# Cross-attention with keys on the partitions: a pass for the maximum, then keys and V as stationary operands in tiles of the array

## The reference, cut to what matters

```python
# x: (2, 1024, 256), context: (2, 154, 256), mask: (2, 154); H = 16 heads of HD = 16
q = split_heads(layernorm(x) @ q_w.T + q_b)
k = split_heads(context @ k_w.T + k_b)
v = split_heads(context @ v_w.T + v_b)
scores = einsum('bhqd,bhkd->bhqk', q, k) / sqrt(HD)
scores = where(mask, -inf, scores)
probs = softmax(scores)
x = x + einsum('bhqk,bhkd->bhqd', probs, v)   # heads side by side again
```

## Time and profile before

| | us |
|---|---|
| median of 3 executions | 926.87 (916.11 to 928.25) |
| profiled execution | 923.59 |
| its span in the trace | 921.8 |
| cross-attention stage, from the first `queries` to the last `head_o` | 500.1 to 690.2 |
[...]

### The profile page before, as it was taken

One profiled execution on the slowest core, in us unless ns is written; L12 is line 12 of the kernel. 1 busy time (PEld: TensorE's weight loads), 2 busy tenths in 40 slices (PEclk: granted clock), 3 DMA queues, 4 the chain that ended last, 5 costly groups with the idle time before them and its releaser, 6 DMA issues.

```text
span 921.8 us, 13568 instructions
## 1 busy us (share of the span) xinstructions
PE 768.8 (83%) x4214; PEld 572.5 (62%) x4215; DVE 508.3 (55%) x1135; ACT 322.0 (35%) x685; POOL 263.9 (29%) x236
## 2 busy tenths in 40 slices
PE   1978661999998684887799999999998479999996
PEld 1733221676766422533366788888888469999995
DVE  5388888565565459223323766666653544444442
ACT  1355642121222220012244655566552022233220
POOL 2754347777776420300000000000000023222231
PEclk9798785899999786778957999999995579999999
DMA  5000001111112162000000000000009201110110
GB/s 173 1 0 0 0 0 34 35 52 34 51 51 52 49 249 116 0 0 0 3 0 1 6 14 12 12 11 11 12 12 325 92 23 33 37 38 30 34 30 1
DMA packets 36210, 37.72 MB, mean 41 GB/s; under 512 B 4648, under 2 KB 32621, under 8 KB 36173
## 3 DMA queue, kind: packets, MB, share of 16 engines
q1 hardware_dynamic: 32956, 32.11, 10.6%
q0 software_dynamic: 2208, 5.12, 1.9%
q10 hardware_dynamic: 1008, 0.03, 0.1%
HBM read 26.77 MB, written 5.11 MB: 35 GB/s over the span
## 4 chain that ended last, share of the span: by engine, by line
PE 61%; issue 16%; DVE 12%; POOL 5%; ACT 3%; DMA 1%; DVEq 0%; SPq 0%; POOLq 0%; ACTq 0%
PE pair L1843 9%; PE bank L1854 9%; PE bank L1736 6%; PE pair L1711 5%; PE bank L1618 4%; PE bank L1724 4%; PE bank L1700 3%; DVE arena L901 3%; PE pair L1433 3%; POOL arena L424 2%; PE bank L1744 2%; PE bank L1807 1%; PE bank L1408 1%; DVE ybuf L1001 1%; POOL arena L409 1%
## 5 line engine op out<-in xcount | busy, mean ns | idle before, releaser
L1433 PE MATMUL pair<-featT,ybuf 128*128 (+1 forms) x128 | 64.9, 666 | 25.3 <-DVE arena L890 24.9
L1182 DVE TENSOR_REDUCE xmax<-pair 128x4 f32<-128x616 f32 x64 | 51.1, 798 | 60.8 <-PE pair L1711 60.8
L1854 PE MATMUL bank<-arena,prob_b 128*128 x368 | 83.1, 379 | 0.0
L1843 PE MATMUL pair<-ybuf 128*128 128x128 f32 x560 | 81.0, 281 | 0.0
L901 DVE SCALAR_TENSOR_TENSOR arena<-arena,conv_w 128x512 f32<-128x512 f32 x72 | 71.5, 1055 | 10.4 <-ACT arena L590 10.3
L1843 PEld LDWEIGHTS pair<-ybuf 128*128 128x128 f32 x560 | 74.5, 198 | 1.1
L505 POOL TENSOR_TENSOR xres<-xres,ybuf 128x256 f32 x16 | 11.6, 724 | 219.1 <-DVE ybuf L1199 219.1
L1854 PEld LDWEIGHTS bank<-arena,prob_b 128*128 128x128 f32 x368 | 68.2, 190 | 8.3
L792 ACT ACTIVATE prob_b<-pair,gate_w 128x128 f32<-128x128 f32 x92 | 26.2, 368 | 117.4 <-PE pair L1843 117.4
L1433 PEld LDWEIGHTS pair<-featT,ybuf 128*128 128x128 f32 x128 | 27.2, 217 | 61.6 <-issue 34.2
L1736 PEld LDWEIGHTS bank<-arena,ybuf 122*128 122x128 f32 x512 | 62.2, 192 | 0.0
(11 more groups left out here) (352 smaller groups left out, 1634.4 us busy)
## 6 DMA issues: line engine op xcount, KB each, us to landing
arena<-W1T SPq DMA_DIRECT2D x8, 1024.0 KB, 12.4
arena<-W2T SPq DMA_DIRECT2D x8, 1024.0 KB, 12.0
arena<-arena SPq DMA_DIRECT2D x16, 384.0 KB, 3.1
xres<-x SPq DMA_DIRECT2D x4, 512.0 KB, 6.6
x_rows<-xres SPq DMA_DIRECT2D x16, 128.0 KB, 1.7
ybuf<-attn_in_wT SPq DMA_DIRECT2D x1, 1288.0 KB, 11.6
featT<-b SPq DMA_DIRECT2D x8, 128.0 KB, 4.7
w_out<-attn_out_wT SPq DMA_DIRECT2D x1, 512.0 KB, 13.0
```

Of the source, the lines that this page charges most:

```text
L1182: dve.tensor_reduce(mx.rearrange("p (a h) -> p a h", a=2), sc, AX, ALU.max).then_inc(S("score_max"), 1)
L1433: m = pe.matmul(bank[f % 5][:, :], w_in[:, k, f * P:(f + 1) * P], featT[:, k, ds(blk * BLK, BLK)], start=(k == 0), stop=(k == KD - 1))
L1843: m = pe.matmul(bank[2 * p + half][:, f * P:(f + 1) * P], w1_now[k][p][:, (4 * half + f) * P:(4 * half + f + 1) * P], xsT[:, p, k, :], sta ...
L1854: m = pe.matmul(bank[4 + p][:, 0:D], hidT[:, p, f, :], w2_of[:, ds(e * NFF + f, 1), :].rearrange("p a n -> p (a n)"), start=(f == 0), stop ...
```

## The change

The maximum is found in a pass of its own. Then the scores are computed a second time with keys as the stationary operand, so that they come out with keys on the partitions, where the weighing needs them; the transposes of probabilities and their copies go. The maximum enters as one more row of the contraction: `neg_max` (the former buffer's column HD + 1, times a constant row of -4 in the key's bias and a scale of 0.25) is transposed and added to the queries, so the second scores are already shifted. Exp reads PSUM directly. V is stationary in 32-column tiles of the array; the output has head columns on the partitions, and is transposed back. `keys` is no longer block-diagonal, so a score matmul uses a 32-row tile of the array, one head each. The tile loops are unrolled in the program text. Some semaphores are merged with shared counters (`dve_once`), which leaves their order as it was.

The diff's core:

```diff
-        pair = [ctx.enter_context(nc.psum_tensor(f"pair{i}", [P, 2, 512], F32)) for i in range(2)]
+        quad = ctx.enter_context(nc.psum_tensor("quad", [P, 4, 512], F32))
-        keys = cut([B, NG, GH * LK])
-        v_main = cut([B, XH, HD + 1])
-        v_tail = cut([B, NG, GH * (HD + 1)])
+        keys = cut([B, NG, LK])
+        key_tail = cut([B, NG, P])
+        v_main = cut([B, XH, 32])
+        v_tail = cut([B, NG, P])
@@ SyncE
-            sp.wait_ge(S("prob_turned"), (NG + 1) * NT)
+            sp.wait_ge(S("pv_mm"), NT)
@@ GpSimd, ahead of the stage
+            pool.memset(bias_rows[:, 1, :, HD + 1:HD + 2], -4.0).then_inc(pool_once, reached("bias_rows_cleared_1"))
+            pool.wait_ge(S("keys_ready"), B * NG)
+            for h in range(GH):
+                r = slice(32 * h, 32 * h + 32)
+                if h:
+                    pool.wait_ge(S("key_tail_ready"), h)
+                pool.tensor_copy(key_tail[r, :, :, 32 * h:32 * h + KT], keys[r, :, :, KM:LK]).then_inc(S("key_tail_ready"), 1)
@@ ScalarE: keys in 8 operations instead of 32, then
+            def exp_scores(t):
+                act.wait_ge(S("main_mm"), t + 1)
+                act.activation(prob_m[0:KM, :, :, :].rearrange("p h g n -> p h (g n)"), quad[0:KM, :, :], ACT.Exp).then_inc(S("prob_m_ready"), 1)
+                act.wait_ge(S("tail_mm"), t + 1)
+                act.activation(prob_t, bank[5][:, :].rearrange("p (g n) -> p g n", g=NG), ACT.Exp).then_inc(S("prob_t_ready"), 1)
+            def keep_o(t):
+                act.wait_ge(S("pv_mm"), t + 1)
+                if t:
+                    act.wait_ge(S("o_turned"), t)
+                act.activation(oT, bank[6][:, :], ACT.Copy).then_inc(S("oT_ready"), 1)
+            for t in range(NT):
+                if t + 2 < NT:
+                    keep_q(t + 2)
+                if t:
+                    keep_o(t - 1)
+                exp_scores(t)
@@ VectorE
+            def max_scores(t, half):
+                dve.wait_ge(S("score_x_mm"), 2 * t + half + 1)
+                for_half = max_cols[:, 2 * half:2 * half + 2, :, HD + 1]
+                dve.tensor_reduce(for_half.rearrange("p g h -> p h g"), quad[:, :, 0:2 * LK].rearrange("p h (g n) -> p h g n", g=2), AX, ALU.max
+                                  ).then_inc(S("score_max"), 1)
+            def add_max(t):
+                dve.wait_ge(S("max_turned"), t + 1)
+                q = qT[:, t % 3, :, :].rearrange("p g n -> p (g n)")
+                dve.tensor_tensor(q, q, bank[7][:, :], ALU.add).then_inc(S("qmax_ready"), 1)
+            # weigh(t): waits o_turned, reads bank[4]; reciprocal and product as before
+            for t in range(NT):
+                if t + 1 < NT:
+                    max_scores(t + 1, 0)
+                    max_scores(t + 1, 1)
+                    add_max(t + 1)
+                if t >= 1:
+                    weigh(t - 1)
+                if t >= 2:
+                    row_stats(t - 2)
@@ TensorE
             def queries(t):
+                if t >= 4:
+                    pe.wait_ge(S("head_o_ready"), t - 3)
+                # 8 matmuls into bank[4]
+            def scores(t, half):
+                if half == 0:
+                    pe.wait_ge(S("qT_ready"), t + 1)
+                    if t >= 2:
+                        pe.wait_ge(S("prob_m_ready"), t - 1)
+                else:
+                    pe.wait_ge(S("score_max"), 2 * t + 1)
+                for i in range(2):
+                    for h in range(GH):
+                        r = slice(32 * h, 32 * h + 32)
+                        m = pe.matmul(quad[:, h, i * LK:(i + 1) * LK], qT[r, t % 3, 2 * half + i, :], keys[r, t // TB, 2 * half + i, :],
+                                      start=True, stop=True)
+            def turn_max(t):       # 4 transposes of neg_max into bank[7]
+            def scores_by_key(t):
+                pe.wait_ge(S("qmax_ready"), t + 1)
+                pe.wait_ge(S("score_max"), 2 * (t + 1) + 2)
+                for g in range(NG):
+                    for h in range(GH):
+                        r = slice(32 * h, 32 * h + 32)
+                        m = pe.matmul(quad[0:KM, h, g * P:(g + 1) * P], keys[r, t // TB, g, 0:KM], qT[r, t % 3, g, :], start=True, stop=True)
+                for g in range(NG):
+                    m = pe.matmul(bank[5][:, g * P:(g + 1) * P], key_tail[:, t // TB, g, :], qT[:, t % 3, g, :], start=True, stop=True)
+            def weigh(t):          # waits prob_m_ready, prob_t_ready, oT_ready
+                for g in range(NG):
+                    pe.matmul(bank[6][:, g * P:(g + 1) * P], v_tail[:, t // TB, g, :], prob_t[:, g, :], start=(g == 0), stop=False,
+                              skip_group_check=True)
+                for g in range(NG):
+                    for h in range(GH):
+                        m = pe.matmul(bank[6][32 * h:32 * h + 32, g * P:(g + 1) * P], v_main[0:KM, t // TB, GH * g + h, :],
+                                      prob_m[0:KM, h, g, :], start=False, stop=True, skip_group_check=True)
+            def turn_out(t):       # waits oT_ready, qT_ready, head_o_ready; 4 transposes of oT into bank[4]
+            queries(0)
+            queries(1)
+            scores(0, 0)
+            scores(0, 1)
+            turn_max(0)
+            for t in range(NT):
+                if t + 1 < NT:
+                    scores(t + 1, 0)
+                if t + 2 < NT:
+                    queries(t + 2)
+                if t + 1 < NT:
+                    scores(t + 1, 1)
+                if t:
+                    weigh(t - 1)
+                scores_by_key(t)
+                if t + 1 < NT:
+                    turn_max(t + 1)
+                if t:
+                    turn_out(t - 1)
+            weigh(NT - 1)
+            turn_out(NT - 1)
```

More of the change, by code:

```diff
@@ L94, in reached @@
             return 1
-        pair = [ctx.enter_context(nc.psum_tensor(f"pair{i}", [P, 2, 512], F32)) for i in range(2)]
-        bank = [pair[i // 2][:, i % 2, :] for i in range(4)]
+        quad = ctx.enter_context(nc.psum_tensor("quad", [P, 4, 512], F32))
+        bank = [quad[:, i, :] for i in range(4)]
         bank += [ctx.enter_context(nc.psum_tensor(f"bank{i}", [P, 512], F32)) for i in range(4, 8)]
@@ L751, in _ @@
-            keep_q(0, 0)
-            def tile_step(t, p, now=True, before=True, waits=True, nxt=True):
-                for g in range(NG):
-                    if nxt and g == 1:
-                        keep_q(t + 1, 1 - p)
-                    if before:
-                        keep_probT(t - 1, g, waits)
-                    if before and g == NG - 1:
-                        keep_probT(t - 1, NG, waits)
-                    if now:
-                        exp_scores(t, p, g)
-            tile_step(0, 0, before=False)
@@ L1276, in _ @@
             link(dve.tensor_reduce(best, hot, AX, ALU.max))
[L1277 removed]
+            dve.tensor_tensor(hot, across(desc, NT), along(best, NE), ALU.is_equal).then_inc(dve_once, reached("hot_ready"))
             link(dve.memset(before[:, 0, :], 0.0))
@@ L1701, in queries @@
                                       start=(k == 0), stop=(k == KD - 1))
                 m.then_inc(S("q_mm"), 1)
-            def scores(t, p, g, waits, b):
-                if waits:
-                    pe.wait_ge(S("shifted"), NG * t + g - 1)
-                if g == 0:
+            def scores(t, half):
+                if half == 0:
                     pe.wait_ge(S("qT_ready"), t + 1)
-                for j in range(2):
-                    r = slice(64 * j, 64 * j + 64)
-                    m = pe.matmul(pair[g % 2][:, j, 0:2 * LK], qT[r, p, g, :],
-                                  keys[r, b, g, 2 * j * LK:(2 * j + 2) * LK], start=True, stop=True)
-                m.then_inc(S("score_x_mm"), 1)
@@ L1730, in weigh_main @@
-            def weigh_main(t, p, g, waits):
-                pe.wait_ge(S("probT_ready"), (NG + 1) * t + g + 1)
-                if g == 0 and waits:
-                    pe.wait_ge(S("head_o_ready"), t - 1)
-                for h in range(GH):
-                    hh = GH * g + h
-                    m = pe.matmul(bank[6 + p][:, hh * W:(hh + 1) * W], probT[0:KM, hh, :],
-                                  vm_of[0:KM, ds((t // TB) * XH + hh, 1), :].rearrange("p a n -> p (a n)"), start=(hh == 0), stop=False,
-                                  skip_group_check=True)
-                m.then_inc(S("pv_mm"), 1)
```

218 lines of the change are left out of this document (75 added, 143 removed).

## The result

| | before | after |
|---|---|---|
| median | 924.91 us (916.11 to 928.25) | 891.17 us (890.72 to 892.75) |
| profiled execution, its span | 923.59, 921.8 | 891.23, 889.5 |
| attention stage, first `queries` to last `head_o` | 190.1 | 157.9 |
| one tile in the steady stretch | 11.68 | 8.90 |
| mean granted TensorE clock of the span, as a share of full speed | 0.874 | 0.879 |

Four executions of each kernel (the median before of three, with which the forecast worked, was 926.87); the ratio is 0.9653, with a 95% interval of 0.9582 to 0.9723. The change makes the program 33.7 us faster. The two spans differ by 32.3: the stage gives 32.2 of it, the part before it took 1.7 more (it begins at 501.87 instead of 500.13) and the part behind it 1.8 less. So the gain is the stage's, as it should be.

What follows compares the result with a forecast made beforehand. PE was taken to bound the attention stage. Its pieces summed to 9.06 us per tile, 9.4 with waits, against 11.68; with the ends this gained 28.9 us, so 926.87 - 28.9 = 898.0, range 885 to 940.

Steps and rivals of the forecast that it cites:

- The bound: Attention stage: PE alone sets the time, 11.68 us per tile before; work taken from VectorE or ScalarE gains nothing by itself.
- The prices: PE's work per tile after the change, priced piece by piece from earlier rows: 9.06 us against 11.68.
- 8 sets of 0.14: V's and keys' tiled matmuls: four tiles overlap, 8 x 0.14 + 0.21 = 1.3 us each per tile.
- Maximum and exponential: VectorE's maximum over 1232 elements takes 1.44 us, ScalarE's exp of 2048 columns 1.9, both extended from shorter operations.
- The waits: Steady tile: queries wait 0.2 us for `head_o`; next scores wait for exp, making the cycle 9.4 us.
- The ends: Fill and drain of the stage: second round starts at about 518.9, last round and drain take 11.2 us.
- rival C, the clock: TensorE's clock makes the changed kernel slower; chance 0.08.
- Edits at nothing: Fewer `keys` writes, GpSimd copies and fills, SyncE's wait, merged semaphores: nothing gained; about 2 us if cover fails.
- A: Tiles overlap only in part, no change: 935 us with serial column tiles, 921 with row tiles two at a time; chance 0.2.
- Column tiles and their loads: V's matmuls in 32-column tiles: priced as overlapping at 1.3 us, between bounds of 1.1 and 3.8.
- B: Small tiles don't overlap at all, held by issue or pass order: cycle 17.2 us, 1015 in all; chance 0.12.
- D: The change does nothing because VectorE or ScalarE set the time; excluded by PE busy 123.0 of 123.0 us.

Runs made afterwards that it cites:

- experiment 5: Kernel after with a second main exponential into a spare buffer ahead of the real one: 918.42 us.
- Experiments 4: Kernel after with the main exponential reading only two of four groups, the other probabilities a constant 0.5: 886.98 us.
- the control: Kernel after, unchanged, run beside three kernels with edited fills (later queries, filler matmuls, both): median 891.63 us, ratio 0.9634 to the kernel before.
- Experiment 1: Kernel after with all sixteen V matmuls of a tile sent to the first 32-column tile: 935.08 us.
- experiment 3: Kernel after with heads outside and groups inside in both tiled loops, so four matmuls in a row use the same tile: 940.1 us.
- the control of experiment 3: Kernel after, unchanged, run beside the kernel with swapped loops: 889.7 us, ratio 0.9613 to the kernel before.
- experiment 2: Kernel after with all second-score matmuls of a tile reading the first head's rows, in one 32-row group: 948.03 us.

## Why the prediction came out right, step by step

**The bound.** PE alone before, PE with small waits after: held. The stage was put at 161.2 and measured 157.9, a gain of 32.2 instead of 28.9; the median at 898.0 and measured 891.2, of which 2.0 are the lower median of the kernel before.

**The prices.** In us per tile:

| term | forecast | measured |
|---|---|---|
| scores, each of two calls | 0.76 | 0.81, 0.74 |
| queries | 1.98 | 2.05 |
| `v_tail`, `key_tail`, each | 1.04 | 1.09 |
| V, 16 matmuls in column tiles | 1.3 | 1.01 |
| keys, 16 matmuls in row tiles | 1.3 | 1.08 |
| 8 transposes | 0.88 | 0.88 |
| PE's sum | 9.06 | 8.75 |
| cycle with waits | 9.4 | 8.90 |

The mis-sized terms are V and the keys, 0.5 together, partly given back by queries and tails (0.17). The rows of the queries and of the first scores hold 0.07 each that is a wait's: behind a wait they take 2.05 and scores 0.81, without one 1.98 and 0.74 (at 524.33 and 523.60 in the chain of the fill, and in experiment 5). So PE's sum free of waits is 8.61, and waits cost 0.29 of the 8.90. V and the keys were both taken as 8 sets of 0.14, a figure worked out from the 0.04 between two loads in the earlier trace rows. The timeline of the kernel after, for passes that start from 590.37 to 590.40, at the start of V's matmuls, shows all four tiles at work, 0.02 apart in their starts and over within 0.32 us:

```profile
590.38 0.32 PE L1746 MATMUL bank<-prob_b,arena 122*32 122x128 f32 x4
```

The next set starts 0.13 later and each one behind it 0.11. So a set costs what a pass of 128 columns costs (0.112), and issuing its four pairs of load and matmul adds nothing. With 0.112 per set the forecast's own formula gives 8 x 0.112 + 0.21 = 1.1 for each, which is what was measured. For the scores the same 0.14 was close, since there a pass is 0.13 long by itself (the first two sets of a call start at 588.78 and 588.92).

**Maximum and exponential.** Both were extended from shorter operations: 1.44 forecast and 1.436 measured, 1.9 and 1.878. That two rows of different length for one operation give a third is the soundest step of the forecast.

**The waits.** Here the forecast was right in size only. It had `queries` waiting 0.2 for `head_o`, hidden later, and then exp setting the cycle, 0.34 above PE's sum. Measured is 0.16, or 0.29 with what a wait adds to the passes behind it. Experiments 4 and 5 show that exp does touch the path (twice the exp costs nearly all of itself), but that it isn't alone: take half of it away, and the shared bank 4 holds the cycle at 8.90. The prediction said what was late next behind PE, and not what was late after that. Its 0.92 from the first scores to `head_o` came out as 0.78 (the product ends at 595.41 in the tile whose scores start at 594.63), and the wait of 0.2 for it as 0.03.

**The ends.** The second round was to start 18.8 us behind the first query. It started 523.60 - 501.87 = 21.7 behind it. Of the 2.9 us, 2.6 are the clock's two falls (the control without them: 19.1). This is rival C, the clock, on a small scale, and the prediction's sum has no term for it. Thirteen cycles took 115.5 (523.60 to 639.13) instead of 122.2 and give back 6.7; the last rounds cost 0.4 more than forecast, with some 1.5 of another fall of the clock in them. So 161.2 + 2.9 - 6.7 + 0.4 = 157.8, the stage as measured but for rounding. That the stage came within 3.3 of the forecast is thus in part luck: cycles priced too high were offset by falls of the clock.

**Edits at nothing.** They held: the stretch ahead of the stage is PE's still, 35.06 of the 37 us from 463 at a granted clock of 0.51 (36.28 and 0.53 in the earlier trace rows), and GpSimd's four copies of 0.39 each are off the chain. The stage begins 1.7 us later in the one profile, but its start moves by 5 us between executions of this same kernel, so the 1.7 can't be put down to the edits.

**The rivals.** A was the right one to fear. Experiment 1 puts its case (column tiles serial) at 935.08, and the prediction's working had 935. So close a hit is luck, for that working starts from 898 and a cycle of 9.4 instead of 891 and 8.90, and 16 times 2.60 makes up for most of it. Its price per pass, 0.112, was put down to a full-array row (whose busy time gives 1.86 / 16 = 0.116, while the starts of its passes lie 0.112 apart in the trace of before, 616.90 to 618.47 for fifteen of them) and holds for a 32-column tile (3.61 / 32 = 0.113). For row tiles that overlap two at a time the working adds 1.5 per tile, where its own prices give 0.49 twice and 0.7, 1.7 together; the time would be 923 or so and not 921, which changes nothing. What decides between A and the forecast is overlap, and experiment 3 adds a condition that the prediction didn't see: it exists only as long as the next passes in program order go to other tiles. B's bound of issue does not exist here: the four tiles of a set start within 0.02 us. For C, whose chance of 0.08 is in the sum, no run shows a stage at the lower clock throughout: in the kernel after the stage was granted 0.84 in its fill, 1.00 in its steady stretch and 0.91 in its last two tiles, and the fill's two falls cost 2.6 us. D was excluded rightly.

**Column tiles and their loads.** The prediction priced V's tiles as overlapping, with no row of before that shows a column tile. The runs show column tiles, which all use the same rows (122 in every pass of V), overlapping fully: 32 passes in 1.01 us against 3.61 in one tile. In experiment 3, where the next tile's first load stands 16 instructions behind its predecessor's first, three passes of eight overlap.

## What to carry to other kernels

Order the instructions of tiled matmuls so that neighbours go to different tiles, and check by the chain of waits that a group of n passes costs n / 4 of a pass, not n; a swap of two loops can cost all of the gain. When a bound falls by a fifth, look for more than the next wait: here two loops of 8.87 and 8.90 lay on top of each other and a third 0.4 behind, so halving one wait gained nothing, and a new order that shortened one loop lengthened another. In fill and drain, where engines work in turn, put independent work of the same engine into the gaps: the gap itself was worth 1.7 us here, and the falls of the clock in the fill, where they came, cost 2.6. That work in the gaps prevents such falls was not shown.

## What the runs showed of the hardware

- Four 32-column tiles with the same rows run side by side, loads included: 32 passes of 128 columns in 1.01 us, against 3.61 in one column tile. Four 32-row tiles: 1.08 against 3.68.
- The overlap depends on program order. With four matmuls (eight passes) in a row to one tile, the next tile starts when five of them have started: 2.39 us (V) and 2.69 us (keys) for the same instructions that take 1.01 and 1.08 in the kernel after (experiment 3).
- A TensorE that is busy 99% (79.23 of 80 us) can still be granted 0.89 on average: experiment 2, where nine of ten falls begin within 0.7 us of the end of a stretch of 3.7 us in one 32-row tile, but not at each of them. In experiment 1, equally busy (78.87 of 80 us), with a stretch of 3.6 us in one 32-column tile, it kept 1.00. The cause is not isolated.
- In the kernel after, work right behind a wait took longer on TensorE: 2.05 instead of 1.98 us for `queries`, 0.81 instead of 0.74 for a call of scores.
- The clock fell to 0.5 in fills and at the end in stretches of 3.4 us: in the fill in two traces of the kernel after (at 513.0 and 519.8, and at 510.4 and 517.2 in the control of experiment 3; 2.6 us lost in each) and not in the third; near the end in all three (at 642.7, 640.1 and 641.6).
